# A down projection by pairs of chunks as seven block products, with one PSUM bank each for the gate and the first layer

## The chip, the core and the metric

The kernel runs on one core of a Trainium2 chip, as one launch. The time is device microseconds from start to end of that launch; lower is better. The engines are TensorE (PE; its weight loads are PEld), VectorE (DVE), ScalarE (ACT), GpSimd (POOL) and SyncE (SP), which issues nearly all transfers.

## What is computed

A batch of four sequences `x` (4, 512 tokens, 256 features) passes two residual layers. In the first, the weight of a sequence is a mix of eight matrices by its `cond_8` row. In the second, a shared gated MLP of width 1024 and two of eight experts, chosen by the same row, are added.

```
def _gemma_mlp(x, gate_w, up_w, down_w):
    g = einsum('bsh,hi->bsi', x, gate_w)
    u = einsum('bsh,hi->bsi', x, up_w)
    return einsum('bsi,ih->bsh', gelu(g, approximate=True) * u, down_w)

# layer 0
w_bot = einsum('bg,got->bot', y, weight * mask)
x = x + einsum('bnt,bot->bno', x, w_bot) + bias
# layer 1: top 2 of softmax(cond_8), renormalised
out = sum over the 2 chosen experts of w_e * _gemma_mlp(x, gate_e, up_e, down_e)
x = x + out + _gemma_mlp(x, shared_gate, shared_up, shared_down)
```

## The kernel before

**Layout.** Features and MLP width lie on the partitions, tokens (T = 512) on the free axis. Everything is fp32, and each product is made of three fp32r products: high by high, high by low, low by high. So every operand is split: ACT rounds it to fp32r (`..._hi`), then DVE or POOL subtracts that from the original (`..._lo`).

**Steps.** A batch is 24 steps `s`: 8 chunks of 128 of the MLP's width for the shared MLP, 8 for the first expert, 8 for the second. A step has 18 matmuls of 512 columns: `gate_up` (L301 to L328) has 6 for the gate into `g_ps[:, s % 2]` and 6 for the up projection into `u_ps[:, s % 2]`, and `down` (L330 to L345) has 6, two output blocks of three, accumulated in `o_ps` over all 24 steps. PE runs `gate_up(s + 2)` and then `down(s)`. Batches 1 and 2 run in a loop on each engine, batch 3 behind it.

**Between them.** ACT makes `gelu`, DVE multiplies (`form_h`, L614, result back in `u_ps`), ACT rounds it to `h_hi`, and DVE subtracts to `h_lo` (`split_h`, L627), always reading `u_ps`. Beside that DVE mixes the next batch's first layer in `l0_ps` (steps 2 to 9), splits `x` (L600) and `x1` (L609), and adds the output (`store_ready`). The first layer of the next batch is 12 matmuls after step 13.

**Expert weights.** SP loads each chunk (gate, up and down, 128x768, 384 KB) into one of eight `raw` slots. Four steps ahead, ACT rounds it (`ex_hi`, L453) and POOL subtracts (`ex_lo`, L721), one instruction of 768 columns per step. POOL does nothing else in the loop.

**The end.** The last three steps of batch 3 go through `final_down` (L347), in 256-column pieces, so that the output can be added and stored piece by piece.

Waits are semaphores written out by hand, and each engine runs its queue in order.

Of the kernel before, what the change touches and what calls it, by code (L numbers as in the profile page):

```python
# [5 lines left out]
P = 128  # L6
F32 = mybir.dt.float32
F32R = mybir.dt.float32r
U32 = mybir.dt.uint32
ALU = mybir.AluOpType  # L10
# [8 lines left out]
RAW_SLOTS = 8  # L19
RING = 8  # L20
H_SLOTS = LAG + 1
SPLIT_LEAD = 4
WARM_UP = 5
L0_STEP = 13


def build(nc, xT, cond, l0_w, l0_mask, experts, shared, outT):
    B, _, HH, T = xT.shape
    G = l0_w.shape[0]
    E, CHUNKS, _, WC = experts.shape  # L30
# [13 lines left out]

    assert RAW_SLOTS == CHUNKS == RING and STEPS % 2 == 0 and STEPS % H_SLOTS == 0 and G == E == 8 and FIRST + SPLIT_LEAD + 1 == CHUNKS

    with ExitStack() as ctx:
# [11 lines left out]
        ones = sb("ones", [1, P])  # L61
# [66 lines left out]
        raw_in = [sem(f"raw_in{i}") for i in range(RAW_SLOTS)]  # L128
# [41 lines left out]

        block = ctx.enter_context(nc.Block())

        @block.sync
        def _(sp):
# [3 lines left out]
            def load_x(b):  # L178
                if isinstance(b, int) and b == 1:
                    sp.wait_ge(x_hi_done, HH)  # L180
                    sp.wait_ge(x_lo_done, HH)
                else:
                    sp.wait_ge(x1_done, HH * b)
                for hh in range(HH):
                    load_x_half(b, hh)

# [3 lines left out]
            def load_expert(b, j, e):  # L190


                sp.wait_ge(w_lo_done, ECH * b + CHUNKS + j - RAW_SLOTS + 1)
                src = experts[bass.ds(e, 1), j % CHUNKS].rearrange("a p w -> (a p) w")
                sp.dma_start(raw[:, j % RAW_SLOTS], src).then_inc(raw_in[j % RAW_SLOTS], 16)
# [3 lines left out]

            def batch(b, with_next):  # L200

                if with_next and not isinstance(b, int):
                    load_x(b + 1)
                e = expert_of(b, 1)
                for j in range(CHUNKS, ECH):
                    load_expert(b, j, e)
                if with_next:
                    e = expert_of(b + 1, 0)
                    for j in range(CHUNKS):
                        load_expert(b + 1, j, e)  # L210
# [574 lines left out]
```

## Time and profile before

| | |
|---|---|
| median of 3 runs | 421.93 us (421.92 to 422.65) |
| the profiled execution, its time | 422.23 us |
| its span | 420.1 us |
| PE busy | 415.3 us, 99% |
| DVE, ACT, POOL busy | 189.7, 184.7, 140.3 us |

The profile gives one execution. Its span is from first to last instruction; the 2.1 us between it and the time are outside. A row of instructions names line, engine, operation and tiles, then times. Matmul durations overlap, so the distance between two starts is what a matmul costs PE.

### The profile page before, as it was taken

How to read it: one execution, taken by the hardware profiler on the slowest of the kernel's cores; microseconds unless marked ns; L12 is line 12 of the kernel's file. 1: busy time of each engine (PE TensorE's matmuls, PEld its weight loads, DVE VectorE, ACT ScalarE, POOL GpSimd, SP SyncE). 2: the span in 40 equal slices, each digit the busy share in tenths (PEclk: the TensorE clock that was granted, in tenths of full speed). 3: DMA queues.
4: the chain of work that ended last, by engine and by line, in shares of the span. 5: the costliest groups of instructions: out<-in, count | busy, mean ns of one | idle time of the engine just before them, and what ended most of it. 6: DMA issues, size and time to landing. Idle time of an engine off the chain costs nothing.

```text
span 420.1 us, 5339 instructions
## 1 busy us (share of the span) xinstructions
PE 415.3 (99%) x1827; PEld 342.5 (82%) x1827; DVE 189.7 (45%) x300; ACT 184.7 (44%) x306; POOL 140.3 (33%) x86
## 2 busy tenths in 40 slices
PE   8999999999999999999999999999999999999997
PEld 6778888888888888888888888888888888888886
DVE  3567744353345455444344545524434433333434
ACT  5676454453324545345232554534422445354421
POOL 1566535343001354535100335443300053444500
PEclk9999999999999999999999999999999999999999
DMA  7964332312011323223102132322300123210001
GB/s 272 352 196 158 100 109 79 114 62 89 0 51 49 101 87 107 81 75 111 39 0 101 37 112 75 112 79 71 112 0 0 51 75 113 76 37 0 2 0 50
DMA packets 14849, 35.05 MB, mean 83 GB/s; under 512 B 1650, under 2 KB 3186, under 8 KB 14834
## 3 DMA queue, kind: packets, MB, share of 16 engines
q1 hardware_dynamic: 14544, 34.61, 24.9%
q10 hardware_dynamic: 290, 0.26, 0.2%
q8 instruction: 7, 0.11, 0.1%
q14 instruction: 8, 0.07, 0.0%
HBM read 32.77 MB, written 2.10 MB: 83 GB/s over the span
## 4 chain that ended last, share of the span: by engine, by line
PE 96%; DMA 1%; DVE 1%; SPq 1%; issue 0%; ACT 0%; DVEq 0%
PE o_ps L342 30%; PE g_ps L321 21%; PE u_ps L321 21%; PE u_ps L327 10%; PE g_ps L327 10%; DMA l_raw<-l_w 1%; PE l_ps L286 1%; PE l_ps L291 1%; PE l_ps L270 0%; DVE l_first L560 0%; PE l_ps L357 0%; SPq L188 0%; DVE out_sb L653 0%; PE l_ps L274 0%; SPq L176 0%
## 5 line engine op out<-in xcount | busy, mean ns | idle before, releaser
L721 POOL TENSOR_TENSOR ex_lo<-raw,ex_hi 128x768 fp32r<-128x768 f32 x64 | 123.4, 1929 | 240.7 <-ACT ex_hi L453 240.7
L444 ACT ACTIVATE gelu<-g_ps 128x512 f32<-128x512 f32 x96 | 57.4, 598 | 175.6 <-PE g_ps L327 175.4
L624 DVE SCALAR_TENSOR_TENSOR u_ps<-gelu,route_cur,u_ps 128x512 f32<-128x512 f32 x64 | 48.3, 755 | 125.5 <-ACT gelu L444 125.5
L629 DVE TENSOR_TENSOR h_lo<-u_ps,h_hi 128x512 fp32r<-128x512 f32 x96 | 66.3, 691 | 31.6 <-ACT h_hi L456 30.5
L456 ACT CAST h_hi<-u_ps 128x512 fp32r<-128x512 f32 x96 | 56.4, 588 | 37.1 <-DVE u_ps L619 18.5
L453 ACT CAST ex_hi<-raw 128x768 fp32r<-128x768 f32 x64 | 52.9, 826 | 0.0
L321 PE MATMUL g_ps<-x_hi,ex_hi 128*128 (+1 forms) x128 | 49.8, 389 | 0.0
L321 PE MATMUL g_ps<-x_hi,ex_lo 128*128 (+1 forms) x128 | 49.8, 389 | 0.0
L321 PE MATMUL u_ps<-x_hi,ex_hi 128*128 (+1 forms) x128 | 49.8, 389 | 0.0
L321 PE MATMUL u_ps<-x_hi,ex_lo 128*128 (+1 forms) x128 | 49.8, 389 | 0.0
L342 PE MATMUL o_ps<-h_hi,ex_hi 128*128 128x512 f32 x122 | 47.5, 389 | 0.0
L342 PE MATMUL o_ps<-h_lo,ex_hi 128*128 128x512 f32 x122 | 47.5, 389 | 0.0
L342 PE MATMUL o_ps<-h_hi,ex_lo 128*128 128x512 f32 x122 | 47.5, 389 | 0.0
L619 DVE TENSOR_TENSOR u_ps<-gelu,u_ps 128x512 f32<-128x512 f32 x32 | 22.2, 695 | 43.7 <-ACT gelu L444 43.7
L327 PE MATMUL u_ps<-x_lo,ex_hi 128*128 (+1 forms) x128 | 39.4, 389 | 0.0
L327 PE MATMUL g_ps<-x_lo,ex_hi 128*128 (+1 forms) x128 | 39.4, 389 | 0.0
L321 PEld LDWEIGHTS g_ps<-x_hi,ex_hi 128*128 128x128 f32 x128 | 24.0, 188 | 5.0
L321 PEld LDWEIGHTS u_ps<-x_hi,ex_lo 128*128 128x128 f32 x128 | 24.0, 188 | 5.0
L327 PEld LDWEIGHTS g_ps<-x_lo,ex_hi 128*128 128x128 f32 x128 | 24.0, 188 | 5.0
L321 PEld LDWEIGHTS u_ps<-x_hi,ex_hi 128*128 128x128 f32 x128 | 24.0, 188 | 5.0
L321 PEld LDWEIGHTS g_ps<-x_hi,ex_lo 128*128 128x128 f32 x128 | 24.0, 188 | 5.0
L327 PEld LDWEIGHTS u_ps<-x_lo,ex_hi 128*128 128x128 f32 x128 | 24.0, 188 | 5.0
(119 smaller groups left out, 561.6 us busy)
## 6 DMA issues: line engine op xcount, KB each, us to landing
raw<-experts SPq DMA_DIRECT2D x64, 384.0 KB, 2.9
raw<-shared SPq DMA_DIRECT2D x8, 384.0 KB, 8.2
l_raw<-l_w SPq DMA_DIRECT2D x8, 256.0 KB, 6.0
x_in<-xT SPq DMA_DIRECT2D x8, 256.0 KB, 4.3
outT<-out_sb SPq DMA_DIRECT2D x8, 128.0 KB, 2.0
outT<-out_sb SPq DMA_DIRECT2D x3, 256.0 KB, 2.1
mask<-l_mask SPq DMA_DIRECT2D x2, 128.5 KB, 6.2
outT<-out_sb ACTq DMA_DIRECT2D x2, 128.0 KB, 2.0
```

The source lines that it names most:

```text
L286: pe.matmul(l0_ps[:, oh], w[:, at:at + P], x_hi[:, th], start=(th == 0 and w is l0_hi), stop=False)
L291: mm = pe.matmul(l0_ps[:, oh], l0_hi[:, at:at + P], x_lo[:, th], start=False, stop=(th == HH - 1))
L321: pe.matmul(ps, w[:, at:at + P], x1_at(x1_hi, b, hh), start=(hh == 0 and w is w_hi), stop=False)
L327: mm = pe.matmul(ps, w_hi[:, at:at + P], x1_at(x1_lo, b, hh), start=False, stop=(hh == HH - 1))
L342: mm = pe.matmul(o_ps[:, oh], w[:, at:at + P], x[:, s % H_SLOTS], start=(s == 0 and i == 0), stop=((closes or s == STEPS - 1) and i == 2))
L444: act.activation(gelu[:, s % 2], g_ps[:, s % 2], ACT.Gelu_apprx_tanh).then_inc(gelu_done, 1)
L453: act.copy(ex_hi[:, j % RING], raw[:, j % RAW_SLOTS]).then_inc(w_hi_done, 1)
L456: act.copy(h_hi[:, s % H_SLOTS], u_ps[:, s % 2]).then_inc(h_hi_done, 1)
L619: dve.tensor_tensor(u_ps[:, s % 2], gelu[:, s % 2], u_ps[:, s % 2], ALU.mult).then_inc(h_done, 1)
L624: dve.scalar_tensor_tensor(u_ps[:, s % 2], gelu[:, s % 2], route_cur[:, k:k + 1], u_ps[:, s % 2], ALU.mult, ALU.mult).then_inc(h_done, 1)
L629: dve.tensor_tensor(h_lo[:, s % H_SLOTS], u_ps[:, s % 2], h_hi[:, s % H_SLOTS].bitcast(F32), ALU.subtract).then_inc(h_lo_done, 1)
L721: pool.tensor_tensor(lo, raw[:, slot], hi.bitcast(F32), ALU.subtract).then_inc(w_lo_done, 1)
```

## The change

In batches 1, 2 and 3 (but for the last two pairs of batch 3) the down projection takes two chunks together. The weights of a pair are a 2 by 2 grid of 128x128 blocks (A11, A12, A21, A22: two output halves by two chunks), and `h` of the pair is a 2 by 2 grid of 128x256 blocks (B: two chunks by two token halves). Seven block products take the place of eight (21 matmuls of 256 columns for 12 of 512), with sums of blocks as operands: S1 to S4 of weights, T1 to T4 of `h`. The products P1 to P7 are accumulated apart in four half banks of `o_ps` and three of `p_ps` over the batch, and combined once at its end.

What this moves:
- `h` of an even step goes to SBUF (`h_a`), no longer back to `u_ps`. DVE forms T1 from `h_a`, then T3, T2 and T4 with `u_ps`. ACT and DVE split T1 to T4 in one instruction of 1024 columns each, beside B11 (256) and B21, B22 (512).
- POOL forms S1 to S4 (four of 128 columns, the last two waiting for earlier ones) for every expert pair, and splits the down weights in two pieces (384 and 512 columns); ACT's rounding of the second piece waits for S4. The splits of `x` and `x1` go from DVE to POOL. At the end of batches 1 and 2 POOL makes the output sums (`sum_products`: 1024, 768, 512, 512, 512 columns) from copies that ACT takes out of PSUM.
- Gate and first layer have one bank each, since the products fill the others. A step's whole gate now comes ahead of its up projection and waits for the step before's `gelu`. The first layer is two halves, after steps 13 and 16.
- Weights are loaded as 256 KB pieces, in 4 slots for gate and up and 2 for down. In batch 0, the down projection is plain; the S blocks of the shared weights are formed at its end from down weights loaded again.

```
+            def product(ps, wt, ht, blk, hf, first, last):
+                for i, (w, h) in enumerate(((0, 0), (0, 1), (1, 0))):
+                    mm = pe.matmul(ps, block_of(wt[w], blk), half_of((h_hi, h_lo)[h], hf), start=(first and i == 0), stop=(last and i == 2))
+                return mm
+            def products_123(b, p):
+                wait_d(b, p)
+                pe.wait_ge(h_lo_done, STEPS * b + 2 * p + 2)
...
+            def products_4567(b, p):
+                pe.wait_ge(t_lo_done, pair_count(b, p) + 1)
...
+            def split_t(b, p):
+                dve.wait_ge(t_hi_done, pair_count(b, p) + 1)
+                at = slice(T1 * TH, 7 * TH)
+                dve.tensor_tensor(h_lo[:, at], t_raw[:], h_hi[:, at].bitcast(F32), ALU.subtract).then_inc(t_lo_done, 1)
...
+            def form_s(count, w):
...
+                pool.tensor_tensor(out(S1), blk(A21), blk(A22), ALU.add).then_inc(s_raw_done, 1)
+                pool.tensor_tensor(out(S3), blk(A11), blk(A21), ALU.subtract).then_inc(s_raw_done, 1)
+                pool.wait_ge(s_raw_done, 4 * count + 1)
+                pool.tensor_tensor(out(S2), out(S1), blk(A11), ALU.subtract).then_inc(s_raw_done, 1)
+                pool.wait_ge(s_raw_done, 4 * count + 3)
+                pool.tensor_tensor(out(S4), blk(A12), out(S2), ALU.subtract).then_inc(s_raw_done, 1)
```

DVE, two steps of a middle batch, around steps 12 and 13, first before and then after (`x_lo`, `l0_lo`, `x1` are work for the next batch):

```order
L624 SCALAR_TENSOR_TENSOR u_ps<-gelu,route_cur,u_ps 128x512 [waits u_done,gelu_done]
L596 TENSOR_TENSOR l0_lo<-l0_ps,l0_hi 128x512 [waits l0_hi_done]
L629 TENSOR_TENSOR h_lo<-u_ps,h_hi 128x512 [waits h_hi_done]
L616 REGISTER_ALU
L624 SCALAR_TENSOR_TENSOR u_ps<-gelu,route_cur,u_ps 128x512 [waits u_done,gelu_done]
L600 TENSOR_TENSOR x_lo<-x_in,x_hi 128x512 [waits x_hi_done]
L629 TENSOR_TENSOR h_lo<-u_ps,h_hi 128x512 [waits h_hi_done]
```

```order
L1007 SCALAR_TENSOR_TENSOR h_a<-gelu,route_cur,u_ps 128x512 [waits u_done,gelu_done]
L1037 TENSOR_TENSOR h_lo<-t_raw,h_hi 128x1024 [waits t_hi_done]
L1016 TENSOR_TENSOR t_raw<-h_a 128x256 [waits h_done,t_lo_done]
L1027 TENSOR_TENSOR h_lo<-h_a,h_hi 128x256 [waits h_hi_done]
L978 REGISTER_ALU
L986 SCALAR_TENSOR_TENSOR u_ps<-gelu,route_cur,u_ps 128x512 [waits u_done,gelu_done]
L1032 TENSOR_TENSOR h_lo<-u_ps,h_hi 128x512 [waits h_hi_done]
L1019 TENSOR_TENSOR t_raw<-u_ps,h_a 128x256
L1020 REGISTER_ALU
L1021 TENSOR_TENSOR t_raw<-u_ps,t_raw 128x256 [waits t_done]
L1022 REGISTER_ALU
L1023 TENSOR_TENSOR t_raw<-u_ps,t_raw 128x256 [waits t_done]
```

The main work of two steps was four DVE instructions, all with an operand in PSUM; now it is nine, of which L1037, L1016 and L1027 have all their operands in SBUF.

POOL, in the loop over middle batches, before (one step) and after (a pair of steps between 8 and 17):

```order
L721 TENSOR_TENSOR ex_lo<-raw,ex_hi 128x768 [waits w_hi_done]
L720 REGISTER_ALU
```

```order
L1239 TENSOR_TENSOR ed_lo<-raw_d,ed_hi 128x384 [waits d_hi_done]
L1240 REGISTER_ALU
L1241 TENSOR_TENSOR ed_lo<-s_raw,ed_hi 128x512 [waits s_hi_done]
L1199 REGISTER_ALU
L1200 TENSOR_TENSOR eg_lo<-raw_g,eg_hi 128x512 [waits gu_hi_done]
...
L1210 TENSOR_TENSOR s_raw<-raw_d 128x128 [waits d_lo_done]
L1211 TENSOR_TENSOR s_raw<-raw_d 128x128
L1212 ISA
L1213 TENSOR_TENSOR s_raw<-s_raw,raw_d 128x128 [waits s_raw_done]
L1214 REGISTER_ALU
L1215 TENSOR_TENSOR s_raw<-raw_d,s_raw 128x128 [waits s_raw_done]
```

Two instructions of 768 columns per pair became eight: 384, 512, 512, 512 and four of 128 (the second L1200 is left out above).

ACT, the same pair of steps after:

```order
L740 ACTIVATE gelu<-g_ps 128x512 [waits g_done]
L762 ISA
L764 CAST h_hi<-t_raw 128x1024 [waits down_done,t_done]
L720 CAST ed_hi<-raw_d 128x384 [waits down_done,raw_d_in1]
L721 ISA
L722 CAST ed_hi<-s_raw 128x512 [waits s_raw_done]
L706 ISA
L711 CAST eg_hi<-raw_g 128x512 [waits u_done,raw_g_in0]
L754 CAST h_hi<-h_a 128x256 [waits down_done,h_done]
L739 REGISTER_ALU
```

L722 is new as a wait of ACT for POOL; behind it in the queue stand the roundings of gate, up and B11 and then the next `gelu`.

## Rows read from the trace of the kernel before

**Rows 1.** The page: span and busy time; granted clock of PE in 40 slices.
```profile
span 420.1 us, 5339 instructions
PE 415.3 (99%) x1827; PEld 342.5 (82%) x1827; DVE 189.7 (45%) x300; ACT 184.7 (44%) x306; POOL 140.3 (33%) x86
PEclk9999999999999999999999999999999999999999
```

**Rows 2.** The page: the chain that ended last, by engine.
```profile
PE 96%; DMA 1%; DVE 1%; SPq 1%; issue 0%; ACT 0%; DVEq 0%
```

**Rows 3.** The same chain in order of time (start us, us, what): two successive `down`.
```profile
396.43 1.36 PE o_ps L342 x6
400.51 1.36 PE o_ps L342 x6
```

**Rows 4.** Timeline of PE, last steps: first, second and last of 36 matmuls of `final_down`.
```profile
412.59 0.28 PE L357 MATMUL l_ps<-h_hi,ex_hi 128*128 128x256 f32 x1
412.70 0.28 PE L357 MATMUL l_ps<-h_lo,ex_hi 128*128 128x256 f32 x1
...
416.78 0.28 PE L357 MATMUL u_ps<-h_hi,ex_lo 128*128 128x256 f32 x1
```

**Rows 5.** Groups by line and form (busy us, mean ns, idle before it): DVE, ACT, POOL.
```profile
L624 DVE SCALAR_TENSOR_TENSOR u_ps<-gelu,route_cur,u_ps 128x512 f32<-128x512 f32 x64 | 48.3, 755 | 125.5 <-ACT gelu L444 125.5
L574 DVE TENSOR_TENSOR l_lo<-l_first,l_hi 128x256 fp32r<-128x256 f32 x2 | 0.8, 420 | 0.1
L600 DVE TENSOR_TENSOR x_lo<-x_in,x_hi 128x512 fp32r<-128x512 f32 x8 | 5.5, 685 | 0.0
L453 ACT CAST ex_hi<-raw 128x768 fp32r<-128x768 f32 x64 | 52.9, 826 | 0.0
L407 ACT CAST x_hi<-x_in 128x512 fp32r<-128x512 f32 x8 | 5.0, 621 | 1.4 <-DMA x_in<-xT 1.4
L721 POOL TENSOR_TENSOR sh_lo<-raw,sh_hi 128x768 fp32r<-128x768 f32 x5 | 9.2, 1849 | 4.2 <-ACT sh_hi L423 4.2
L725 POOL TENSOR_TENSOR sh_lo<-raw,sh_hi 128x256 fp32r<-128x256 f32 x6 | 4.3, 739 | 13.5 <-ACT sh_hi L427 13.5
```

**Rows 6.** Timeline of all engines, around 62 us: DVE with two SBUF operands, then POOL.
```profile
62.75 0.68 DVE L600 TENSOR_TENSOR x_lo<-x_in,x_hi 128x512 fp32r<-128x512 f32 x1
62.85 2.29 POOL L721 TENSOR_TENSOR ex_lo<-raw,ex_hi 128x768 fp32r<-128x768 f32 x1 [2.24 <-ACT ex_hi L453]
```

**Rows 7.** The same around 42 us: POOL, then DVE instructions of 8 and 512 columns.
```profile
42.29 0.17 DVE L542 TENSOR_SCALAR pair_rest<-pair 128x8 f32<-128x8 f32 x1
42.45 1.84 POOL L721 TENSOR_TENSOR ex_lo<-raw,ex_hi 128x768 fp32r<-128x768 f32 x1 [2.23 <-ACT ex_hi L453]
42.49 1.82 DVE L544 SCALAR_TENSOR_TENSOR route_w<-pair,pair_rest 128x8 f32<-128x8 f32 x1
```

**Rows 8.** Timeline, one step of a middle batch around 202 us, DVE and ACT.
```profile
201.53 0.60 ACT L444 ACTIVATE gelu<-g_ps 128x512 f32<-128x512 f32 x1 [2.07 <-PE g_ps L327]
202.16 0.75 DVE L624 SCALAR_TENSOR_TENSOR u_ps<-gelu,route_cur,u_ps 128x512 f32<-128x512 f32 x1 [1.98 <-ACT gelu L444]
202.95 0.59 ACT L456 CAST h_hi<-u_ps 128x512 fp32r<-128x512 f32 x1 [0.82 <-DVE u_ps L624]
203.57 0.69 DVE L629 TENSOR_TENSOR h_lo<-u_ps,h_hi 128x512 fp32r<-128x512 f32 x1 [0.65 <-ACT h_hi L456]
```

**Rows 9.** Timeline of the start: first `gelu`, and PE from the first step to the second.
```profile
18.99 0.60 ACT L444 ACTIVATE gelu<-g_ps 128x512 f32<-128x512 f32 x1 [0.23 <-PE g_ps L327]
18.79 0.62 PE L327 MATMUL u_ps<-x_lo,sh_hi 128*128 128x512 f32 x2
19.25 0.39 PE L321 MATMUL g_ps<-x_hi,sh_hi 128*128 128x512 f32 x1
```

**Rows 10.** The page: transfers (KB each, median us from issue to landing).
```profile
raw<-experts SPq DMA_DIRECT2D x64, 384.0 KB, 2.9
```

More of the change, by code:

```diff
@@ L18 @@
 FIRST = 3
-RAW_SLOTS = 8
 RING = 8
-H_SLOTS = LAG + 1
+RAW_G = 4
+RAW_D = 2
+RING_D = 2
 SPLIT_LEAD = 4
 WARM_UP = 5
-L0_STEP = 13
+EVAC_SEED = 6
+A11, A12, A22, A21, S1, S2, S3, S4 = 0, 1, 2, 3, 3, 4, 5, 6
+B11, B21, B22, T1, T3, T2, T4 = 0, 1, 2, 3, 4, 5, 6
 def build(nc, xT, cond, l0_w, l0_mask, experts, shared, outT):
@@ L322, in gate_up @@
-                for (ps, off), done in ((gate, g_done), (up, u_done)):
-                    for hh in range(HH):
-                        if s == 0 and off == GATE:
-                            pe.wait_ge(x1_lo_done, HH * b + hh + 1)
-                        at = off + hh * P
-                        mm = pe.matmul(ps, w_hi[:, at:at + P], x1_at(x1_lo, b, hh), start=False, stop=(hh == HH - 1))
-                    mm.then_inc(done, 1)
-            def down(b, s):
+                    pe.wait_ge(gu_lo_done, gu_index(b, s - CHUNKS) + 1)
@@ L394, in _ @@
             first_layer_0()
-            for s in range(LAG):
-                gate_up(0, s)
-            with pe.Fori(0, B - 1) as b:
+            first_gate_up()
+            gate_up(0, 1)
+            batch(0, True)
+            with pe.Fori(1, B - 1) as b:
                 batch(b, True)
@@ L675, in beside, with step @@
-                    if s in (L0_STEP + 4, L0_STEP + 5):
-                        split_x1(b + 1, s - L0_STEP - 4)
-            def batch(b, with_next):
-                for s in range(1, STEPS):
-                    if not with_next and s == STEPS - 1:
-                        add_rest()
+                    if s in (16, 20):
+                        residual(b + 1, (s - 16) // 4)
+            def step(b, s, with_next):
+                p = s // 2
+                if not fast(b, p):
+                    form_h(b, s)
+                    if s % 2 == 0 and s > 0 and fast(b, p - 1):
+                        split_t(b, p - 1)
+                    beside(b, s, with_next)
+                    split_h(b, s)
+                elif s % 2 == 0:
+                    form_a(b, p)
+                    if p > 0 and fast(b, p - 1):
+                        split_t(b, p - 1)
+                    beside(b, s, with_next)
+                    form_t1(b, p)
+                    split_b11(b, p)
+                else:
@@ L707, in _ @@
             route_index()
-            form_h(0, 0)
-            split_h(0, 0)
+            for s in range(2):
+                step(0, s, False)
             batch(0, True)
@@ new lines, in batch @@
+            def batch(b, with_next):
+                for s in range(2, STEPS):
+                    if s >= CHUNKS and s % 2 == 0:
+                        split_d(b, (s - CHUNKS) // 2)
+                    if s < 2 + ECH:
+                        split_gu(b, s - 2)
+                    q = (s - CHUNKS + 1) // 2
+                    if s % 2 and 0 <= q < EPR and fast(b, PAIRS + q):
+                        expert_s(b, q)
+                    if with_next:
+                        next_beside(b, s)
+                if with_next:
+                    sum_products(b)
@@ L747 @@
+                split_up(c)
+            split_shared_d(0)
+            for i in range(1, PAIRS):
+                for c in range(2 * i + 1, min(2 * i + 3, CHUNKS)):
+                    split_shared(c)
+                if i < PAIRS - 1:
+                    split_shared_d(i)
+            batch_0()
+            with pool.Fori(1, B - 1) as b:
+                batch(b, True)
+            batch(B - 1, False)
 def kernel(**inputs):
```

899 lines of the change are left out of this document (668 added, 231 removed).

## The prediction

> **What bounds the kernel now.** I read the page's busy times first: PE is at 99%, the others are at 33 to 45% [rows 1]. The chain of waits agrees, 96% of it PE with nothing else over 1% [rows 2]. In the chain by time, `down` comes every 4.08 us [rows 3]; a step has 18 matmuls of 512 columns, so one costs PE 0.2267 us, and there is no gap. The other engines wait for PE: only work taken off PE can gain, and it gains only while the others still keep up. PE's granted clock is at its upper level (2.4 GHz) throughout [rows 1].
>
> **1. PE's work.** The 36 matmuls of 256 columns at the end start from 412.59 to 416.78, 35 distances of 0.1197 us [rows 4]: two of them cost 0.239, 6% more than one of 512. Down costs 12 x 0.2267 = 2.72 us per pair of steps before and 21 x 0.1197 = 2.51 after. The gain is 0.206 us per pair (not the 0.34 of an eighth), over 12 + 12 + 10 pairs of batches 1, 2, 3: **7.0 us**. A pair then takes PE 7.95 us (8.16 before): P123 1.08, gate and up 2.72, P4567 1.44, gate and up 2.72. Batch 0's steps cost PE what they did.
>
> **2. The start.** The gate of step 1 began at 19.25, right behind step 0's matmuls; the first `gelu` ran from 18.99 to 19.59 [rows 9]. The single gate bank makes PE wait for it: +0.35 us, with the smaller loads I take **+0.5**. Later gates find `gelu` done unless ACT falls behind: the up projection and a product stand between them.
>
> **3. The loop through DVE and ACT.** Before, a step asked DVE for 0.755 + 0.69 us [rows 5, 8] of 4.08, up to 0.75 more with work for the next batch. Let B be the end of `h_lo` for B21 and B22, which releases P123. I add durations [rows 5], with 0.03 us from engine to engine and 0.08 less between neighbours on one engine, as in rows 8. DVE forms T3, T2, T4 (256 columns, 0.42; T4 waits for T2): B + 1.1. ACT rounds 1024 columns, by the step from 512 to 768 an estimated 1.03: A = B + 2.2, `form_a` beside it. DVE subtracts 1024 columns (from 256 and 512, 1.22), to A + 1.25; T1, then B11's low part. At F, `form_h` begins; 0.755 + 0.59 + 0.69 and hand-overs later B comes again, F + 2.1. If nothing is in the way, F = A + 1.9 and the loop takes 6.2 us; PE needs 7.95, and DVE waits for it. Slack is at most about 1.4 us, since `form_a` needs an up projection that PE does late.
>
> **4. POOL in the way.** This decides. When DVE subtracted two SBUF tiles at 62.75, POOL's instruction of 768 columns, asked for at 62.85, took 2.29 us instead of 1.84 [rows 6]. At 42.49 a DVE instruction of 8 columns with its operands in SBUF took 1.82 us and ended 0.02 after POOL's (42.45 + 1.84); its neighbour with one took 0.17 [rows 7]. So an instruction of DVE with two operands in SBUF and one of POOL exclude each other. Hand-over comes some 0.15 us before the recorded end, both ways (65.14 - 1.84 = 63.30 against 63.43; 44.31 - 0.17 = 44.14 against 44.29). Before, DVE did this four times a batch. Now it does it three times per pair (the 1024 subtraction, T1, B11), and POOL, by 739 ns for 256 and 1849 for 768 columns [rows 5] at 1.02 (384), 1.30 (512) and 0.46 (128), does 1.02 + 3 x 1.30 + 4 x 0.46 = 6.8 us per pair in steps 8 to 17. With DVE's 1.22 + 2 x 0.42 that is 8.8, less 6 hand-overs and the overlaps of neighbours 7.9 to 8.0, against PE's 7.95: **the pair of engines is full there**.
>
> In order: DVE's 1024 subtraction (to A + 1.25), POOL's 384 (which asked at A + 0.45, while T1 waits for DVE's subtraction to end; to A + 2.13), T1 (2.40), POOL's 512 (3.56), B11 (3.83). F = A + 3.8, so the loop takes 2.2 + 3.8 + 2.1 = 8.1 us, 0.13 over PE, in all pairs from step 8 on. The slack eats that: 1.0 in a batch. The first layer's matmuls cost PE what they did (two halves of 1.36) and give slack at steps 13 and 16. On top come:
> - the two splits of `x` on POOL (1.30 each, after steps 9 and 11): S4 comes late, ACT stands for it with B11's rounding behind, and the loop takes some 9.1 and 9.4 us in two pairs (one with a half of the first layer). Net of slack +0.4 in batch 1, +1.8 with the decay in batch 2, which starts without slack.
> - the output sums on POOL at the start of batches 2 and 3: 2.41 + 1.85 + 3 x 1.30 = 8.2 us by the same two rows. DVE gets its three turns only between them; worked through, the first pair's loop takes 10.5, the second 8.8, the third 8.4 (POOL catching up): with 1.86 of slack at the batch boundary, where POOL is idle, **+1.9** in each batch.
> - batch 3 has no next batch, but no slack from a first layer either: 7 pairs at 0.13, +0.9.
>
> Stalls: 0.4 + (1.9 + 1.8) + (1.9 + 0.9) = **6.9 us**. Where batch 1 and 2 hide DVE work for the next batch (0.69 to 0.75), it lies under POOL's 384 columns.
>
> The Trainium skill (SBUF - State Buffer, "Who interferes with whom") says that a DVE instruction with two SBUF inputs contends with a GpSimd instruction that reads SBUF, and that the loser is blocked for the whole instruction. The trace agrees on who blocks whom; rows 6 and 7 put the hand-over 0.15 us ahead of the recorded end. By whole instructions the loop would be the 8.7 us of rival B.
>
> **5. The end.** DVE has the six additions of the products (about 4.6 us) in the steps before the last; worked through, the last `h_lo` comes about 1 us after PE wants it, where before it came in time: **+1.0** (0 to 2).
>
> **6. Loads.** 256 KB pieces with fewer slots: a slot is free two steps or more before its next content is rounded, against 2.9 us for 384 KB [rows 10]. Nothing, up to +1.
>
> **The sum,** from the profiled execution's 422.23 (span 420.1): -7.0 + 0.5 + 6.9 + 1.0 = +1.4, so 423.6; the median of the runs lies 0.3 below it: **423.3 us**. The gain is certain and small; nearly the same amount goes again where DVE and POOL exclude each other.
>
> **Rivals.**
> - **A: the cover holds** (chance 0.33). If DVE keeps its turn from T1 to B11, POOL's 512 columns (1.15 net) fall out of the loop: 6.9 us, the stalls at sums and splits shrink to about 1.5, and 421.9 - 7.0 + 0.5 + 1.5 + 0 to 1.0 gives 417 to 418; with no stalls at all 415.5. For it: POOL as second loser is not shown anywhere. Against it: where POOL had one instruction behind another and DVE waited, DVE got in between, and I see no reason for another rule the other way round.
> - **B: slower, whole instructions** (0.17). If the 0.15 us at each hand-over isn't to be had when turns follow closely, the loop is 2.2 + 4.4 + 2.1 = 8.7 us from step 8 on and 8.9 before it once slack is gone. It decides as soon as the loop passes 7.95. 0.7 us in 22 pairs more is +15: 437 us.
> - **C: another price** (0.05): the 256-column products run slower with their waits, or PE's clock falls in the gaps; each 10 ns per product matmul is 34 x 21 x 0.01 = +7 us: 430.
> - That the products' gain isn't there: as the matmuls are plain instructions of a form that the trace has, no chance of its own.
>
> **How the numbers follow.** My forecast has 0.45, 420 to 427: each 0.1 us on the loop is about +2 us (22 pairs), and the terms above carry that uncertainty; about 0.05 of it is faster and 0.10 within 0.2%, which is about what a measurement of this kernel can tell from no change. With A (0.33, 415 to 420) faster is 0.38; same 0.10; slower 0.30 + 0.17 + 0.05 = 0.52. The range from 416 to 434 leaves out A's lower edge (0.05) and most of B's upper half with C (0.12).
>
> **What would show it.** Product matmuls 0.12 us apart, pairs of 7.95 us where PE is not stalled. In the pairs of steps 8 to 17, POOL's 384 and 512 between DVE's 1024, T1 and B11, with records longer than their work (T1 near 1.3 us rather than 0.42), and PE idle in front of P123 for `h_lo`. The largest gaps (2 us or so) in steps 0 to 5 of batches 2 and 3 while `sum_products` runs, and around step 12 of batch 2; ACT waiting for POOL there. Batch 1 nearly free of stalls. If B11 follows T1 at once, it is A; if every pair has 0.7 us or more of PE idle, it is B. I am wrong altogether if PE waits for loads or for `gelu`, or if DVE and POOL overlap freely.

## The result

| | before | after |
|---|---|---|
| median | 421.95 us (421.92 to 422.65, 4 runs) | 427.61 us (426.85 to 428.24, 4 runs) |
| span of the profiled execution | 420.1 us | 426.0 us |
| PE busy | 415.3 us, 99% | 414.5 us, 97% |
| DVE, ACT, POOL busy | 189.7, 184.7, 140.3 us | 318.6, 223.9, 273.3 us |

The ratio after to before is 1.0129, with a 95% interval of 1.0108 to 1.0151: the change makes the kernel 1.3% slower. The forecast was 423.3 us (416 to 434), with slower as the likeliest sign.

The page of the kernel after, for [rows 1] and [rows 2]: span, busy times, granted clock, and the chain that ended last by engine.

```profile
span 426.0 us, 6965 instructions
PE 414.5 (97%) x2133; PEld 349.1 (82%) x2133; DVE 318.6 (75%) x459; ACT 223.9 (53%) x407; POOL 273.3 (64%) x271
PEclk9999999999999999999999999999999999999999
PE 66%; DVE 18%; issue 9%; ACT 4%; DMA 1%; SPq 1%; DVEq 0%; ACTq 0%
```

The clock is as before. PE's share of the chain fell from 96% to 66%: the end is now set by a loop that goes through DVE and ACT. DVE is busy 129 us longer and POOL 133, and neither comes near the whole span, so the busy shares do not show that these two are full. The durations of the groups do (busy us, mean ns of one, idle before it):

```profile
L1037 DVE TENSOR_TENSOR h_lo<-t_raw,h_hi 128x1024 fp32r<-128x1024 f32 x34 | 51.8, 1525 | 6.5 <-ACT h_hi L764 6.4
L1016 DVE TENSOR_TENSOR t_raw<-h_a 128x256 f32<-128x256 f32 x34 | 31.7, 933 | 0.6
L1021 DVE TENSOR_TENSOR t_raw<-u_ps,t_raw 128x256 f32<-128x256 f32 x34 | 14.1, 415 | 0.0
L1027 DVE TENSOR_TENSOR h_lo<-h_a,h_hi 128x256 fp32r<-128x256 f32 x34 | 45.3, 1333 | 0.6 <-ACT h_hi L754 0.6
L1239 POOL TENSOR_TENSOR ed_lo<-raw_d,ed_hi 128x384 fp32r<-128x384 f32 x22 | 36.8, 1671 | 22.1 <-ACT ed_hi L720 22.1
```

Three of these DVE groups have 256 columns. L1021, with one operand in PSUM, takes 415 ns, near the 420 of [rows 5]. T1 (L1016) and B11's low part (L1027), with both operands in SBUF, are recorded at 933 and 1333 ns: more than half of these records is waiting. POOL's 384 columns, 1.02 us of work by the step from 256 to 768 columns in [rows 5], are recorded at 1.67.

### Where the time went

PE's first matmul behind the first step of each batch cuts the span into batches. The timeline of PE in the kernel before has these at 24.99, 125.63, 226.27 and 326.91, 100.64 us apart. In the kernel after they are at:

```profile
125.95 0.38 PE L563 MATMUL p_ps<-h_hi,sd_hi 128*128 128x256 f32 x1
227.76 0.28 PE L563 MATMUL p_ps<-h_hi,sd_hi 128*128 128x256 f32 x1
331.87 0.28 PE L563 MATMUL p_ps<-h_hi,sd_hi 128*128 128x256 f32 x1
414.43 0.39 PE L556 MATMUL l_ps<-x_hi,ed_hi 128*128 128x512 f32 x1
```

The last of these is step 20 of batch 3, at 408.51 before. From one P123 to the next, a pair of steps that does not stall takes 8.00 us, and 9.36 with half of the next batch's first layer in it. The pairs of batch 1 took 8.09, 8.21, 8.35, 8.08, 9.14, 9.15 and 9.43, then 8.00 (once 9.36); those of batch 2 took 10.28, 8.36, 8.35, 8.07, 9.15, 9.12 and 9.42, then the same; those of batch 3 took 8.92, 8.83, 8.29, then 8.07 or 8.08. A batch without stalls would take 12 x 8.00 + 2 x 1.36 = 98.72 us. This gives the whole account:

| term | forecast | measured | worked out as |
|---|---|---|---|
| PE's work | -7.0 | -5.4 | (98.72 - 100.64) x 2, and 80.0 - 81.60 for ten pairs |
| start and batch 0 | +0.5 | +0.3 | 125.95 - 125.63 |
| stalls of batch 1 | +0.4 | +3.1 | 101.81 - 98.72 |
| stalls of batch 2 | +3.7 | +5.4 | 104.11 - 98.72 |
| stalls of batch 3 | +2.8 | +2.6 | 82.56 - 80.0 |
| end | +1.0 | 0.0 | 11.57 - 11.59 |
| sum | +1.4 | +5.9 | before rounding of the terms; 426.0 - 420.1 = +5.9 |

### How DVE and POOL take turns

The timeline of DVE and POOL over one pair of steps in batch 3 (start us, us, then as above):

```profile
376.15 1.23 DVE L1037 TENSOR_TENSOR h_lo<-t_raw,h_hi 128x1024 fp32r<-128x1024 f32 x1 [0.34 <-ACT h_hi L764]
376.61 1.65 POOL L1239 TENSOR_TENSOR ed_lo<-raw_d,ed_hi 128x384 fp32r<-128x384 f32 x1 [0.49 <-ACT ed_hi L720]
377.41 1.13 DVE L1016 TENSOR_TENSOR t_raw<-h_a 128x256 f32<-128x256 f32 x1
378.22 1.48 POOL L1241 TENSOR_TENSOR ed_lo<-s_raw,ed_hi 128x512 fp32r<-128x512 f32 x1
378.46 1.51 DVE L1027 TENSOR_TENSOR h_lo<-h_a,h_hi 128x256 fp32r<-128x256 f32 x1
```

This is the order of the prediction's step 4: DVE's 1024 columns, POOL's 384, T1, POOL's 512, B11. Taking the plain duration of an instruction off its recorded end gives the time at which its work began. POOL's 384 began at 378.26 - 1.02 = 377.24, 0.14 us before DVE's record ends at 377.38. T1 began at 378.54 - 0.42 = 378.12, 0.14 before 378.26. B11 began at 379.97 - 0.42 = 379.55, 0.15 before 379.70. So the hand-over 0.15 us ahead of the recorded end, read from [rows 6, 7], holds in a close sequence too. The pairs here take 8.08 us; the forecast loop was 8.1.

The Trainium skill (SBUF - State Buffer, "Who interferes with whom") speaks of the loser as blocked for the whole instruction. The trace agrees on who blocks whom; by the three numbers above, the blocking ends 0.14 to 0.15 us before the record does.

### The profile page after: what moved, and what is told of

Read it like the earlier page. It is cut to its first block, busy times and chain, and to the rows that moved or that the text cites. A ratio compares the mean times of both kernels' runs of the same rounds, so it can differ in the third digit from the quotient of the medians.

```text
span 426.0 us, 6965 instructions
## 1 busy us (share of the span) xinstructions
PE 414.5 (97%) x2133; PEld 349.1 (82%) x2133; DVE 318.6 (75%) x459; ACT 223.9 (53%) x407; POOL 273.3 (64%) x271
## 4 chain that ended last, share of the span: by engine, by line
PE 66%; DVE 18%; issue 9%; ACT 4%; DMA 1%; SPq 1%; DVEq 0%; ACTq 0%
PE o_ps L556 7%; PE g_ps L503 7%; PE g_ps L502 7%; PE g_ps L506 7%; PE u_ps L506 7%; PE u_ps L502 7%; PE u_ps L503 7%; PE o_ps L563 7%; PE p_ps L563 5%; DVE h_lo L1027 4%; ACT h_hi L764 3%; DVE h_lo L1037 2%; PE l_ps L461 2%; DVE l_ps L955 2%; DMA l_raw<-l_w 1%
## 5 line engine op out<-in xcount | busy, mean ns | idle before, releaser
L1200 POOL TENSOR_TENSOR eg_lo<-raw_g,eg_hi 128x512 fp32r<-128x512 f32 x64 | 89.2, 1408 | 43.9 <-ACT eg_hi L711 43.9
L1037 DVE TENSOR_TENSOR h_lo<-t_raw,h_hi 128x1024 fp32r<-128x1024 f32 x34 | 51.8, 1525 | 6.5 <-ACT h_hi L764 6.4
L503 PE MATMUL g_ps<-x_hi,eg_lo 128*128 128x512 f32 (+1 forms) x128 | 50.4, 394 | 0.0
L502 PE MATMUL g_ps<-x_hi,eg_hi 128*128 128x512 f32 (+1 forms) x128 | 50.1, 391 | 0.0
L502 PE MATMUL u_ps<-x_hi,eg_hi 128*128 128x512 f32 (+1 forms) x128 | 49.8, 389 | 0.0
L503 PE MATMUL u_ps<-x_hi,eg_lo 128*128 128x512 f32 (+1 forms) x128 | 49.8, 389 | 0.0
L1027 DVE TENSOR_TENSOR h_lo<-h_a,h_hi 128x256 fp32r<-128x256 f32 x34 | 45.3, 1333 | 0.6 <-ACT h_hi L754 0.6
L506 PE MATMUL g_ps<-x_lo,eg_hi 128*128 128x512 f32 (+1 forms) x128 | 39.6, 390 | 0.0
L506 PE MATMUL u_ps<-x_lo,eg_hi 128*128 128x512 f32 (+1 forms) x128 | 39.4, 389 | 0.0
L1032 DVE TENSOR_TENSOR h_lo<-u_ps,h_hi 128x512 fp32r<-128x512 f32 x34 | 23.5, 691 | 16.8 <-ACT h_hi L759 16.8
L1016 DVE TENSOR_TENSOR t_raw<-h_a 128x256 f32<-128x256 f32 x34 | 31.7, 933 | 0.6
```

Of the source, the lines that this page charges most:

```text
L502: pe.matmul(ps, w_hi[:, at:at + P], x1_at(x1_hi, b, hh), start=(hh == 0), stop=False)
L503: pe.matmul(ps, w_lo[:, at:at + P], x1_at(x1_hi, b, hh), start=False, stop=False)
L506: mm = pe.matmul(ps, w_hi[:, at:at + P], x1_at(x1_lo, b, hh), start=False, stop=(hh == HH - 1))
L1027: dve.tensor_tensor(h_lo[:, 0:TH], h_a[:, 0:TH], h_hi[:, 0:TH].bitcast(F32), ALU.subtract).then_inc(h_lo_done, 1)
L1037: dve.tensor_tensor(h_lo[:, at], t_raw[:], h_hi[:, at].bitcast(F32), ALU.subtract).then_inc(t_lo_done, 1)
L1200: pool.tensor_tensor(eg_lo[:, j % RING], raw_g[:, j % RAW_G], eg_hi[:, j % RING].bitcast(F32), ALU.subtract).then_inc(gu_lo_done, 1)
```

## The experiments

The theory: PE's stalls are turns that DVE's instructions with two SBUF operands lose to POOL. The rivals: the stalls come from the length of the loop through DVE and ACT itself, or from the waits between the engines, whatever POOL does. The medians of the kernel before, on the chips of the three groups of runs, were 421.69, 421.95 and 421.89 us; each ratio is against its own.

### poolnarrow: POOL's splits nearly free

```
-                pool.tensor_tensor(eg_lo[:, j % RING], raw_g[:, j % RAW_G], ...
+                w = W2 if at_first(b) else 16
+                pool.tensor_tensor(eg_lo[:, j % RING, 0:w], raw_g[:, j % RAW_G, 0:w], ...
...
-                form_s(s_count(b, q), raw_d[:, d_slot(b, q)])
+                form_s(s_count(b, q), raw_d[:, d_slot(b, q)], 16)
...
-                    pool.tensor_tensor(ed_lo[:, q % RING_D, S1 * P:7 * P], s_raw[:], ...
+                    pool.tensor_tensor(ed_lo[:, q % RING_D, S1 * P:S1 * P + 16], s_raw[:, 0:16], ...
```

> In batches 1 to 3 GpSimd's splits of expert weights and its S blocks are 16 columns wide (most of those low parts and sums are left out); waits, semaphores, x splits and output sums stay. Theory (GpSimd's instructions block VectorE's instructions with two SBUF operands): T1 (933 ns mean in the changed kernel) and B11's subtraction (1333 ns) fall to about 0.42 us, and all PE gaps go but those beside the output sums (2.3 in batch 2, 0.9 in batch 3): about 420 us. Rival (VectorE just has too much work): 426 us or more, VectorE's instructions as long as they are.

Measured: 421.19 us, ratio 0.9981 (0.9965 to 0.9998), span 418.1. The groups of DVE:

```profile
L1016 DVE TENSOR_TENSOR t_raw<-h_a 128x256 f32<-128x256 f32 x34 | 16.2, 478 | 0.6
L1027 DVE TENSOR_TENSOR h_lo<-h_a,h_hi 128x256 fp32r<-128x256 f32 x34 | 18.8, 553 | 0.6 <-ACT h_hi L754 0.6
```

T1 and B11 fall to 0.48 and 0.55 us, with DVE's own work, all waits and all of ACT's work as they were. Behind its first pair (8.09) batch 1 has no stall left, and nearly all other pairs take 8.00 us, or 9.36 with half of a first layer. That first pair takes 8.09 or 8.10 in every run: PE waits for `h_lo` in front of the first P123 (0.19 us here and in the kernel after), and its first product then costs 0.09 more. PE's only gaps over 0.1 us are 0.49 at the start of step 1's gate, 0.19 in front of the first P123, and 2.28 and 0.92 in the first pairs of batches 2 and 3, where the output sums, which this edit leaves alone, stand in POOL's queue. By the profiled executions 7.9 us of the span went with the width of POOL's instructions alone, by the medians 6.4: six of the ten executions had a mean granted clock of 0.995 or 0.996 and took 421.06 to 421.97 us, the other four, the profiled one among them, one of 1.0 and took 419.18 to 420.19.

The rivals fall: the loop itself fits under PE. Narrow instructions also finish earlier, so ACT or PE could have been waiting for POOL's results rather than DVE for its turn. The trace of the kernel after rules that out for batches 1 to 3: ACT is never idle in front of L722, its one wait for POOL's S blocks there, and none of PE's gaps ends with POOL.

### nocombine: the mixing of the next first layer nearly free

```
-                    dve.tensor_scalar(l0_ps[:], l0_raw[:, g], cond_cur[:, g:g + 1], None, ALU.mult)
+                    w = L0C if isinstance(b, int) and b == 1 else 8
+                    dve.tensor_scalar(l0_ps[:, 0:w], l0_raw[:, g, 0:w], cond_cur[:, g:g + 1], None, ALU.mult)
```

> In batches 1 and 2 the mixing of the next first layer on VectorE is 8 columns wide instead of 512 (most of that mix is left out): 16 instructions of 0.75 us less VectorE work, none of which uses two SBUF operands. Theory (turns between VectorE and GpSimd): they lie under GpSimd's instructions, so at most 0.5 us less, about 427.3. Rival (too much VectorE work): up to 0.75 us less in each of 8 stalled pairs, 421 to 424 us.

Measured: 425.47 us, ratio 1.0090 (1.0073 to 1.0107), between the two expectations. Batch 1 fell from 101.81 to 100.12: its pairs of steps 2 to 7 took 8.00 us, the first pair with a split of `x` took 8.07 instead of 9.14, and only the second kept its gaps (0.57 and 0.41). Batch 2 stayed at 104.03. So the mixing, which the prediction laid under POOL's 384 columns everywhere, is not hidden in steps 2 to 7 of batch 1, and its removal does nothing once the loop of batch 2 has started late.

### yield and ygu: POOL gives way by hand

The first makes POOL wait for B11's low part before its own next instruction, in two places; the second in the first of them only.

```
                 pool.wait_ge(gu_hi_done, gu_index(b, j) + 1)
+                s = j + (SPLIT_LEAD if at_first(b) else 2)
+                if s % 2 and s < CHUNKS and fast(b, s // 2):
+                    pool.wait_ge(h_lo_done, STEPS * b + s)
                 pool.tensor_tensor(eg_lo[:, j % RING], ...
...
                     pool.wait_ge(s_hi_done, s_count(b, q) + 1)
+                    if fast(b, (CHUNKS + 2 * q) // 2):
+                        pool.wait_ge(h_lo_done, STEPS * b + CHUNKS + 2 * q + 1)
                     pool.tensor_tensor(ed_lo[:, q % RING_D, S1 * P:7 * P], ...
```

> GpSimd waits for B11's low part before its second instruction of a pair (the S part of the down split; in steps 2 to 7 the odd step's gate and up split), so VectorE has T1 and B11 in one turn. Nothing is left out. Theory: B11's subtraction falls from 1.33 us mean to under 0.6, the loop through VectorE from 8.08 to about 7 us, pairs go from 8.08 and 8.35 to 8.00; GpSimd's total stays, so the pairs with a split of x still stall: 422.5 us (421 to 425). Rival (GpSimd is saturated, order is no matter): 427 to 429.

> Only the half of the turn rule that concerns steps 2 to 7: in the odd step GpSimd waits for B11's low part before it splits gate and up weights. Nothing is left out. Theory (in those steps GpSimd takes the turn between T1 and B11 only because the odd step's gate is done early, when PE has no slack; once PE has slack it stays): pairs of 8.21 and 8.35 in batch 1 become 8.00, PE arrives at step 8 with over 1 us of slack, which then takes up a part of the x splits: batch 1 100 us (101.8 in the changed kernel), batch 2 103.2, in all 424.2 us. Rival (slack is given back, the total of GpSimd decides): 427.

Measured: yield 425.77 us, ratio 1.0082 (1.0055 to 1.0110), 3 us worse than expected; ygu 424.23 us, ratio 1.0054 (1.0039 to 1.0069), as expected. In both, the pairs of steps 2 to 7 of batch 1 take 8.00 us; batch 1 takes 100.01 and 100.07. In yield the record of B11 falls from 1.33 to 0.57 us on average, as expected. Yet the second wait, in steps 8 to 17, gives nothing in batch 1 and costs in batch 3, where it takes 74.98 us from the first P123 to the last, against 73.12 in ygu. Some 1.6 us of the profiled execution of yield have another cause: its granted clock was 0.69 from 236 to 240 us, behind the 2.27 us gap of batch 2, and the pair there took 9.66 us (8.07 in ygu). The timeline of yield in batch 3, POOL, ACT and PE:

```profile
385.35 1.29 POOL L1246 TENSOR_TENSOR ed_lo<-s_raw,ed_hi 128x512 fp32r<-128x512 f32 x1 [1.10 <-DVE h_lo L1027]
...
392.03 0.62 ACT L722 CAST ed_hi<-s_raw 128x512 fp32r<-128x512 f32 x1 [2.04 <-POOL s_raw L1218]
394.12 0.47 PE L502 MATMUL g_ps<-x_hi,eg_hi 128*128 128x512 f32 x1 [0.52 <-ACT gelu L740]
```

B11 gets its turn at once, but POOL stands 1.10 us for it, which it does not have, and comes late with the next S4. ACT stands for that 2.04 us at L722, with the next `gelu` queued behind, and PE waits for that `gelu` in front of the single gate bank. The stall has moved from P123 to the gate, and in batch 3 it has grown (pairs of 8.20 to 8.74 us, all of 8.00 in ygu). The view of waits lists it 15 times (who waits for whom: us in total, times, longest us), and does not list it in the kernel after:

```profile
ACT ed_hi L722 <- POOL s_raw L1218: 27.2, 15, 2.1
```

Where POOL has room (steps 2 to 7) giving way costs nothing; where it is full it did not pay.

### xearly and xearly2: the splits of x where POOL has room

In both, `x` of the next batch is rounded and split some four steps earlier. xearly leaves the loads alone; xearly2 also moves the load of `x` ahead of the loads of gate and up chunks 4 to 6 in SP's queue.

```
-                if s in (8, 10):
-                    split_x(b + 1, (s - 8) // 2)
+                x_at = 8 if at_first(b) else 4
+                if s in (x_at, x_at + 2):
+                    split_x(b + 1, (s - x_at) // 2)
```

> In batches 1 and 2 the next x is rounded in steps 4 and 6 and its low part taken in steps 5 and 7, where GpSimd has room, instead of 8, 10 and 9, 11. Nothing is left out. Theory: the four pairs of 9.15 us (GpSimd's x split directly in front of VectorE's 1024 columns) become 8.08: 4.3 us less, about 423.4. Rival (GpSimd's total of the batch decides): the same 427.6.

> The earlier x split again, with the load of x put ahead of the loads of gate and up chunks 4 to 6 (in the first try ScalarE stood 6 us for that load). ScalarE rounds x in steps 5 and 6, GpSimd subtracts in 5 and 7. Nothing is left out. Theory: the four pairs of 9.15 us around steps 10 to 13 become 8.08, no new gap: 423.4 us. Rival: the time is lost elsewhere in the batch, 426 to 428.

Measured: xearly 438.51 us, ratio 1.0404 (1.0386 to 1.0421), 15 us over the expectation. ACT waited for the load, 7.34 us, and PE for a `gelu` behind it; and when PE came back, it was slow:

```profile
144.10 0.62 ACT L670 CAST x_hi<-x_in 128x512 fp32r<-128x512 f32 x1 [7.34 <-DMA x_in<-xT]
145.27 0.80 PE L502 MATMUL g_ps<-x_hi,sg_hi 128*128 x1 [5.90 <-ACT gelu L740]
145.86 0.63 PE L503 MATMUL g_ps<-x_hi,sg_lo 128*128 x1
146.29 0.63 PE L502 MATMUL g_ps<-x_hi,sg_hi 128*128 x1
```

The table by stretches (from and to, length, busy time of PE, PEld, DVE, ACT and POOL with their instructions, granted clock, DMA share, GB/s) of the same kernel:

```profile
145.00:148.00 3.00, 2.73 (x7) 2.15 (x8) 2.72 (x6) 1.31 (x3) 2.20 (x2) 0.50 0.01 3
150.00:155.00 5.00, 5.00 (x30) 4.37 (x30) 3.84 (x6) 2.32 (x5) 2.02 (x2) 0.97 0.16 54
```

The load of `x` stood in SP's queue behind loads that wait for POOL to free their slots, and those come later than step 4. The miss is in my reading of the queue, not in the theory: I had moved ACT's instruction past the moment at which its input is issued. After 5.9 us without work, PE's next dozen matmuls started 0.43 us apart instead of 0.23, at a granted clock of 0.50, the 1.2 GHz level, and behind them it was back at the upper one. The same happened in batch 2.

xearly2 measured 423.41 us, ratio 1.0039 (1.0025 to 1.0053); expected was 423.4. The pairs with the `x` splits, 9.15 before, take 8.07, and batches 1 and 2 take 99.67 and 102.03, 2.1 us less each. The same POOL instructions cost 2 us a batch in steps 9 and 11 and nothing in steps 5 and 7.

### nosum and latesum: the output sums

nosum makes every output sum 8 columns wide per block. latesum keeps the sums whole and takes ygu's wait, and places them in three parts behind steps 3, 5 and 7 of the next batch, where POOL's queue has least.

```
+                    if b > 1 and s in (3, 5, 7):
+                        sum_products(b - 1, (s - 3) // 2)
...
-                if with_next:
-                    sum_products(b)
-
-            def sum_products(b):
+            def sum_products(b, part):
...
-            with pool.Fori(1, B - 1) as b:
+            for b in range(1, B - 1):
```

> The changed kernel with the output sums of batches 1 and 2 on GpSimd 8 columns wide per block (most of those sums is left out); all waits stay. Theory: the gaps at step 2 of batches 2 (2.3) and 3 (0.9) go, batch 3's later ones shrink since PE keeps its slack: batch 2 about 101.8 instead of 104.1, 427.6 - 2.3 - 2.0 = 423.3 us. Rival (the gap at step 2 comes from the waits around the end of a batch, not from the sums' width): 427.

> As ygu, and the output sums of batches 1 and 2 are made in three parts in steps 3, 5 and 7 of the next batch, each behind GpSimd's split of that step, instead of in one row at its start. Nothing is left out. Theory: the gaps of 2.3 and 0.9 us at step 2 of batches 2 and 3 go, and PE keeps its slack of the batch boundary: batch 2 like batch 1 at about 100, 419 us in all, faster than both kernels. Rival (the sums cost the same wherever they stand, since GpSimd and VectorE are full): 424.

Measured: nosum 421.59 us, ratio 0.9993 (0.9981 to 1.0004); latesum 420.03 us, ratio 0.9957 (0.9943 to 0.9971), a microsecond over its expectation. nosum took 1.7 us more off than expected. Batch 1 is as it was (101.78), but batch 2 falls by 4.1 us to 99.97 and batch 3 runs at 8.00 for its first pairs. The gap at the sums was only 2.3 us; the rest is the slack that now survives and swallows the later late turns, those of the mixing and the first of the `x` splits among them. How the sums held DVE up in the kernel after is in the timeline of DVE and POOL at the start of batch 2:

```profile
227.67 2.42 POOL L1293 TENSOR_TENSOR out_sb<-x,x_in 128x1024 f32<-128x1024 f32 x1 [11.10 <-DVE x L1051]
228.63 2.53 DVE L1037 TENSOR_TENSOR h_lo<-t_raw,h_hi 128x1024 fp32r<-128x1024 f32 x1
230.16 2.71 POOL L1295 TENSOR_TENSOR out_sb<-out_sb,x_in 128x768 f32<-128x768 f32 x1
231.09 1.81 DVE L912 COPY cond_cur<-cond_all 128x8 f32 x1
232.95 1.29 POOL L1297 TENSOR_TENSOR out_sb<-out_sb,x_in 128x512 f32<-128x512 f32 x1
233.70 0.82 DVE L1016 TENSOR_TENSOR t_raw<-h_a 128x256 f32<-128x256 f32 x1
234.44 1.50 DVE L1027 TENSOR_TENSOR h_lo<-h_a,h_hi 128x256 fp32r<-128x256 f32 x1
```

DVE's 1024 columns waited 1.3 us for the first sum. A copy of 8 columns from SBUF to SBUF was recorded at 1.81 us, since it needed a turn as well (the same copy took 0.16 us at 129.09, where POOL was idle); only then came T1 and B11. PE's P123 waited:

```profile
238.04 0.36 PE L563 MATMUL p_ps<-h_hi,sd_hi 128*128 128x256 f32 x1 [2.13 <-DVE h_lo L1032]
```

In latesum this gap and that of batch 3 are gone: batch 3 has no pair above 8.01, and batches 1 and 2 keep only the `x` gaps (0.56 and 0.42; 0.32, 0.41, 0.53 and 0.41). POOL's loop over the batches is unrolled for this edit; that is not what removes the two gaps at the sums, since nosum keeps the loop and loses them too.

### combo: the 8-column copy moved to ACT

```
+                if with_next:
+                    act.wait_ge(masked, HH * b + HH)
+                    act.copy(cond_cur[:], cond_all[:].rearrange("p b e -> p (b e)")[:, bass.ds((b + 1) * G, G)])
...
-                    if s == 2:
-                        pick_cond(b + 1)
```

> latesum with ScalarE picking the next batch's cond row in place of VectorE, whose copy of 8 columns took 1.81 us beside GpSimd at the start of batch 2. Nothing is left out. Theory: that copy needs the turn too, and with the sums spread it still meets GpSimd's split: up to 1 us less than latesum, 418 to 419. Rival: no difference, since the copy lies under another wait.

Measured: latesum with this edit, 420.45 us, ratio 0.9963 (0.9949 to 0.9977), against 0.9957 (0.9943 to 0.9971) without it: no difference. With the sums out of the way the copy costs nothing. Whether it costs what the rows suggest with the sums in place (batch 2's first gap of 2.29 us against batch 3's 0.91, where there is neither copy nor mixing) was not tried alone. It is not the mixing: nocombine has the same first pair in batch 2, 10.27 us.

### xdve: the x split on the engine with the shorter turn

```
+            def first_x_lo_of(b, hh):
+                dve.wait_ge(x_hi_done, HH * b + hh + 1)
+                dve.tensor_tensor(x_lo[:, hh], x_in[:, hh], x_hi[:, hh].bitcast(F32), ALU.subtract).then_inc(x_lo_done, 1)
...
+                    if not at_first(b) and s in (11, 13):
+                        first_x_lo_of(b + 1, (s - 11) // 2)
...
-                if s in (9, 11):
+                if at_first(b) and s in (9, 11):
```

> latesum with the low part of the next x made by VectorE in steps 11 and 13 of batches 1 and 2, as in the kernel before, not by GpSimd in 9 and 11. Nothing is left out. Theory: on VectorE the same subtraction holds the turn for 0.55 us instead of 1.30 and stands where VectorE waits for ScalarE anyway, so the gaps of 0.56, 0.42 (batch 1) and 0.32, 0.41, 0.53, 0.41 (batch 2) go: 417.6 us. Rival (VectorE is as full as GpSimd, the delay only moves to B21/B22's low part): 420.

Measured, on top of latesum: 418.17 us (417.66 to 418.66), ratio 0.9911 (0.9894 to 0.9928). This version beats both kernels, that of before by 0.9%. Batches 1 and 2 take 98.90 and 99.75 us, 1.2 us together over 98.72. Two rows show the trade: the split on POOL in the kernel after, and on DVE in xdve.

```profile
160.69 1.30 POOL L1247 TENSOR_TENSOR x_lo<-x_in,x_hi 128x512 fp32r<-128x512 f32 x1
160.77 2.30 DVE L1037 TENSOR_TENSOR h_lo<-t_raw,h_hi 128x1024 fp32r<-128x1024 f32 x1 [0.18 <-ACT h_hi L764]
```

```profile
164.09 1.12 DVE L946 TENSOR_TENSOR x_lo<-x_in,x_hi 128x512 fp32r<-128x512 f32 x1
```

On POOL, 512 columns hold the turn for about 1.15 us, and here they had it 0.08 us before DVE asked with its 1024; DVE lost the whole of it. On DVE they need 0.69 us [rows 5], the rest of the 1.12 being a wait, and POOL is freed of them in the steps where it is full.

## Why the prediction came out as it did

**Its mechanism held.** It put the loss into turns between DVE and POOL, with the hand-over 0.15 us ahead of the recorded end, and poolnarrow shows that cause by itself. The loop of steps 8 to 17 was 8.08 us where PE had no slack (8.1 forecast); T1 was recorded at 1.13 us (near 1.3); rivals A (B11 directly behind T1) and B (loop 8.7) are both refuted by the rows at 376 to 380. Slower was right, but the sum of +1.4 was 4.5 us short of the +5.9 measured.

**For the splits of `x` the number was near and the path was not.** The forecast had S4 late, ACT standing for it, and loops of 9.1 and 9.4 us in two pairs. In the kernel after ACT never stands for S4: POOL's split has the turn when DVE asks for its 1024 columns (the rows at 160.69 and 160.77), the low part of T1 to T4 comes late, and PE waits for it in front of P4567 (0.37 to 0.41 us) and again in front of the next P123 (0.25). Two pairs take 9.12 to 9.15 us, 1.12 to 1.15 over their 8.00; the third, of 9.42 or 9.43, is only 0.07 over its 9.36. That 9.1 and 9.4 look alike is luck.

**Which instructions need a turn was drawn too narrowly.** The control in [rows 7], the 0.17 us of the neighbour with one operand, had ended at 42.46, when POOL had only just started (42.45), so it showed nothing about one operand; the copy of 8 columns, with one, did wait.

The steps, one by one:

**1. PE's work: -5.4, not -7.0.** The 21 products do cost 0.1197 us each. But a 512-column matmul behind a run of 256-column ones costs more than 0.2267. The timeline of PE after, last product and the next gate:

```profile
204.71 0.28 PE L563 MATMUL o_ps<-h_hi,ed_lo 128*128 128x256 f32 x1
204.83 0.40 PE L502 MATMUL g_ps<-x_hi,eg_hi 128*128 x1
205.06 0.40 PE L503 MATMUL g_ps<-x_hi,eg_lo 128*128 x1
...
206.22 0.39 PE L502 MATMUL u_ps<-x_hi,eg_hi 128*128 x1
```

The first six take 206.22 - 204.83 = 1.39 us, 0.232 each, so +0.03 twice a pair: 8.00 instead of 7.95, and a gain of 0.16 per pair instead of 0.206. The term assumed that the two widths have their own prices in any order; the trace of the kernel before could not show it, since its 256-column products all stand at the end. What causes it stays open.

**2. The start: +0.3 (+0.5).** The gap in front of step 1's gate is there, 0.49 us, and ended by `gelu` as forecast.

**3. The loop without POOL** fits: in poolnarrow batch 1 has no stall behind its first pair.

**4. Batch 1: +3.1, not +0.4. This is the term that was mis-sized most.** The slack on which "batch 1 nearly free of stalls" rests was nearly gone in its first pair. The turns there, in the kernel after:

```profile
126.79 1.30 POOL L1200 TENSOR_TENSOR eg_lo<-raw_g,eg_hi 128x512 fp32r<-128x512 f32 x1 [11.96 <-ACT eg_hi L711]
126.82 2.35 DVE L1037 TENSOR_TENSOR h_lo<-t_raw,h_hi 128x1024 fp32r<-128x1024 f32 x1
...
129.40 0.76 DVE L952 TENSOR_SCALAR l_ps<-l_raw,cond_cur 128x512 f32<-128x512 f32 x1 [0.15 <-DVE cond_cur L912]
129.89 1.29 POOL L1200 TENSOR_TENSOR eg_lo<-raw_g,eg_hi 128x512 fp32r<-128x512 f32 x1 [1.79 <-ACT eg_hi L711]
130.07 1.39 DVE L1016 TENSOR_TENSOR t_raw<-h_a 128x256 f32<-128x256 f32 x1
```

POOL, idle for 11.96 us, asked 0.03 us before DVE, and DVE's 1024 columns were 1.1 us late at once. That alone does not decide: ygu and nocombine have the same collision, 2.35 us included, and their next pairs take 8.00. The second loss does. The mixing (L952) stands in front of T1, so POOL's split of the odd step asks 0.18 us before T1 and T1 is 1.0 us late. The `h_lo` for the second P123 then ends 0.3 us before PE gets there (133.74 against 134.04); in ygu, where POOL waits, it ends 1.3 us before, and in nocombine 1.8. With so little slack left, the gate and up split of the odd step takes the turn ahead of B11 in steps 2 to 7 as well:

```profile
144.91 1.82 POOL L1200 TENSOR_TENSOR eg_lo<-raw_g,eg_hi 128x512 fp32r<-128x512 f32 x1 [5.03 <-ACT eg_hi L711]
146.93 1.51 DVE L1027 TENSOR_TENSOR h_lo<-h_a,h_hi 128x256 fp32r<-128x256 f32 x1
```

So the loop is 8.35 us there. That costs 0.7 us in the first four pairs (0.09 of it stands in every run), and the `x` splits, 2.4 us, then fall on a loop with nothing to give; the forecast had counted both against slack. The prediction worked such late turns out only for batches 2 and 3, whose first steps it saw late. ygu measures it: with POOL giving way in these steps, batch 1 takes 1.7 us less, since the first `x` split is then absorbed, 8.03 us instead of 9.14; and nocombine, which takes the mixing out of DVE's side, gives the same 1.7.

**Batch 2: +5.4, not +3.7.** At the sums the forecast had a first loop of 10.5 us less 1.86 of slack, so 8.64 from P123 to P123. Batch 3 took 8.92; batch 2 took 10.28. What batch 2 has and batch 3 has not, DVE's work for the next batch, was left out of the sum, the 8-column copy with its 1.81 us above all. In batch 3 T1 has the turn behind the sum of 768 columns and ends 5.40 us after the P123; in batch 2 the copy has that turn, and T1 ends 6.76 us after it. The 1.36 us between them are those between 8.92 and 10.28. This is read from the rows and not shown by a run of its own. The three pairs at the sums cost 3.0 us (1.9 forecast), those at the `x` splits 2.3 (1.8). **Batch 3: +2.6 (+2.8)** is right in both halves: 2.0 at the sums (1.9), and 7 pairs at 0.08 (0.13) behind them.

**5. The end: 0, not +1.0.** The last `h_lo` came just in time:

```profile
420.55 0.69 DVE L992 TENSOR_TENSOR x_lo<-u_ps,x_hi 128x512 fp32r<-128x512 f32 x1 [0.65 <-ACT x_hi L748]
421.38 0.36 PE L605 MATMUL o_ps<-x_hi,ed_hi 128*128 128x256 f32 x1
```

The final matmuls that do not need it started from 418.51 to 421.26, and the first that does at 421.38; 421.24, the end of `h_lo`, lies within them. **6. Loads** cost nothing, as forecast.

## What to carry to other kernels

Where two engines exclude each other, draw up who has the turn when, instruction by instruction; their busy shares (75% and 64% here) did not show it, and an added instruction of 8 columns was held for a whole turn of the other. In a loop as long as its period (8.1 us against 8.00) slack decides more than any single price: lost once at the start of a batch, it made 1.7 us (batch 1, ygu) and 1.9 us (batch 2, nosum) of later stalls appear that the same work did not cause with slack in hand, so work out the turns of the very first pair. And the cure is place, not force: the same POOL work cost nothing a few steps earlier or on the engine that holds the turn for less time, while a wait that holds the full engine back only moved the stall, and an instruction moved ahead of its input's place in a load queue made the kernel 11 us slower.

## What the runs showed of the hardware that was not expected

- **The width before matters to PE.** Six 512-column matmuls behind a run of 256-column ones start 0.232 us apart, not 0.2267.
- **A restart costs.** When PE waits in front of a P123, its first product is recorded at 0.36 us instead of 0.28 and the second starts 0.20 after it, not 0.12. Pairs that wait just barely are 8.08 us, not 8.00. In the kernel after, batch 3:

```profile
365.98 0.36 PE L563 MATMUL p_ps<-h_hi,ed_hi 128*128 128x256 f32 x1
366.18 0.28 PE L563 MATMUL p_ps<-h_lo,ed_hi 128*128 128x256 f32 x1
```

- **A gap can take the clock with it.** After the 5.9 us gap of xearly a dozen matmuls ran at a granted clock of 0.50, 0.43 us apart. In yield seven distances of 0.43 followed the 2.27 us gap in batch 2; the 2.29 us gap in the kernel after was followed by none.
- **0.03 us can decide a turn.** POOL at 126.79 and DVE at 126.82 began within 0.03 us of each other, and DVE's 1.22 us of work took 2.35.
- **A copy with one SBUF operand needs the turn too.** 8 columns took 0.16 us with POOL idle (129.09) and 1.81 us beside POOL's sum of 768 columns (231.09).
